# GpSimd's low part and division beside VectorE's block maxima, scales in one pass, column products in an earlier step

## The reference

```
Q = xn Wq^T + bq ; K = xn Wk^T + bk ; V = xn Wv^T + bv
Q, K divided by their norms over the 2048 tokens (per feature)
tailor = 1 / (256 + Q . (sum of K over features + 1e-6))
s = xn + gamma * tailor * (sum of V + Q (K^T V))          # linear attention
g = silu( ffn(xn) ),  ffn(x) = fp4_linear( silu(fp4_linear(x, w_gate)) * fp4_linear(x, w_up), w_down )
out = x + s * g
```

## Time and profile before

| | us |
|---|---|
| median of 3 runs | 691.5 |
| the three runs | 691.96, 686.57, 691.5 |
| the profiled execution | 686.41 |
| its span, first to last instruction | 684.5 |
| mean granted clock of PE | 0.984 |

### The profile page before, as it was taken

The page is one execution under the profiler, slowest core; times in us unless marked ns, Lnnn a source line. Parts: engine busy times, 40 slices in busy tenths (PEclk is TensorE's granted clock), DMA queues, the critical chain, the costliest instruction groups (busy, mean ns, idle before and its releaser), DMA issues.

```text
span 684.5 us, 14876 instructions
## 1 busy us (share of the span) xinstructions
PE 582.3 (85%) x4845; PEld 439.9 (64%) x4845; DVE 612.0 (89%) x1221; ACT 418.6 (61%) x1046; POOL 288.4 (42%) x224
## 2 busy tenths in 40 slices
PE   0247788999999699999999779999998889999767
PEld 0134566677768476777767656777776666777656
DVE  7987999999989999999989989999989998887634
ACT  3157887867667577766666567766667575553410
POOL 5424334443541335554752533554752443133315
PEclk9999999999999999999999999999999999999988
DMA  7001100000001001111101111111100110140123
GB/s 234 0 15 32 32 18 16 16 18 16 16 17 32 32 1 47 47 49 48 47 10 40 47 49 47 47 48 47 47 18 31 48 32 32 32 139 32 33 78 124
DMA packets 17758, 29.38 MB, mean 43 GB/s; under 512 B 2704, under 2 KB 5136, under 8 KB 17680
## 3 DMA queue, kind: packets, MB, share of 16 engines
q1 hardware_dynamic: 17680, 28.39, 12.5%
HBM read 19.99 MB, written 8.39 MB: 41 GB/s over the span
## 4 chain that ended last, share of the span: by engine, by line
DVE 48%; PE 25%; issue 18%; ACT 4%; POOL 2%; DMA 1%; DVEq 1%; SPq 0%; POOLq 0%; ACTq 0%
PE GU L1300 10%; DVE hg L863 5%; DVE h L823 5%; DVE hq L871 4%; DVE ham L830 4%; DVE hs L853 4%; PE G L1352 4%; DVE st L779 3%; PE DS L1311 3%; DVE xt L805 2%; DVE xq L814 2%; DVE y L882 2%; DVE ht L860 2%; DVE xg L808 2%; DVE xss L792 1%
## 5 line engine op out<-in xcount | busy, mean ns | idle before, releaser
L1300 PE MATMUL GU<-wgu,xqT 128*128 128x352 f16 x1536 | 256.5, 318 | 9.1 <-DVE h L823 4.6
L1300 PEld LDWEIGHTS GU<-wgu,xqT 128*128 128x128 f16 x1536 | 149.7, 100 | 85.5 <-ACT xnT L596 7.4
L520 POOL TENSOR_TENSOR ht<-h,hrr 128x1408 f32<-128x1408 f32 x32 | 82.9, 2590 | 238.7 <-DVE hrr L837 238.3
L580 ACT ACTIVATE sil<-GU,wkap 128x352 f32<-128x352 f32 x128 | 70.9, 555 | 105.0 <-PE GU L1300 103.2
L823 DVE SCALAR_TENSOR_TENSOR h<-GU,wkap,sil 128x352 f32<-128x352 f32 x128 | 72.0, 562 | 30.0 <-ACT sil L580 27.0
L1311 PE MATMUL DS<-wdT,hqT 128*128 128x256 f16 x704 | 88.2, 274 | 4.6 <-DVE y L882 3.3
L1311 PEld LDWEIGHTS DS<-wdT,hqT 128*128 128x128 f16 x704 | 66.7, 98 | 14.1 <-DVE y L882 3.3
L587 ACT COPY hqT<-TR 128x768 f16<-128x768 f16 x64 | 51.1, 798 | 32.6 <-PE TR L1258 32.0
L871 DVE TENSOR_TENSOR hq<-hg,hs 128x704 f16<-128x704 f16 x128 | 64.3, 544 | 1.0
L487 POOL TENSOR_TENSOR xt<-xs,xrr 128x512 f32<-128x512 f32 x32 | 43.5, 1360 | 42.2 <-DVE xrr L796 42.2
L1258 PE MATMUL TR<-id,hq 128*128 128x128 f16 x704 | 51.3, 220 | 7.9 <-ACT xnT L596 7.5
(11 more groups left out here) (181 smaller groups left out, 1095.8 us busy)
## 6 DMA issues: line engine op xcount, KB each, us to landing
xin<-in_L_attn_x SPq DMA_DIRECT2D x34, 256.0 KB, 2.7
xe<-in_L_attn_x SPq DMA_DIRECT2D x25, 256.0 KB, 2.9
out<-o SPq DMA_DIRECT2D x25, 256.0 KB, 2.1
h<-in_L_ffn_w_down SPq DMA_DIRECT2D x1, 704.0 KB, 6.5
gring<-in_L_ffn_w_gate SPq DMA_DIRECT2D x1, 640.0 KB, 4.5
gring<-in_L_ffn_w_up SPq DMA_DIRECT2D x1, 640.0 KB, 5.2
xs<-in_L_attn_x SPq DMA_DIRECT2D x2, 256.0 KB, 4.0
xt<-in_L_attn_x SPq DMA_DIRECT2D x2, 256.0 KB, 4.7
```

The lines of the kernel that those rows point to most:

```text
L520: g.tensor_tensor(paired(ht[:, 0:2 * I]), paired(h[:, q]), spread(hrr[:, q], 4 * CB), ALU.mult).then_inc(S["ht_d"], 1)
L580: a.activation(sil[:, c], GU[:, c, 0, 0:CH], ACT.Silu, scale=wkap[:, 0:1]).then_inc(S["sil_d"], 1)
L1300: last = t.matmul(GU[:, c, m, 0:CH], xqT[:, k, j, 2 * a_ + kc], wgu[:, b_, kc, 2 * m + c], start=(i == 0 and kc == 0), stop=(i == 2 and kc ...
```

## The change

Five edits:
- `h_high` (ScalarE) writes the scaled scales in f32 to a new tile `hsp` (still two operations of 44 columns), waits for them, and copies all 88 columns to `hs1`. VectorE's `h_parts(2)` is one operation hsp*1.0 - hs1 on 88 columns. Semaphore counts follow.
- POOL's `x_low` and `x_divide` go to the end of the iteration and wait for `hloq` = 2p, the last `hq` product of the iteration, behind which VectorE has the block maxima L830, then L834 and L837.
- POOL's `norm_products` run in step 3 (step 2 in the last batch), behind ht and ahead of o.
- `x_shift` is made by two ScalarE operations at the head of `x_norm`; VectorE's L792 moves behind the second `h` of the iteration, directly ahead of L796.
- "cols" is asked in (1, 0, 2) and answered in (1, 1, 0), in place of (3, 0, 0) and (3, 0, 1); turn moves to (1, 1, 1) and (1, 1, 2), t1q to (2, 0, 1), norms to (3, 1, 0). Waits of turn, cols and norms follow.

```diff
+        hsp = sb("hsp", [P, 2 * HB])
-        ASKS = {..., (1, 1, 0): "turn", (2, 0, 0): "t1q", (2, 1, 0): "t1k", (3, 0, 0): "cols", (3, 0, 2): "norms", ...
+        ASKS = {..., (1, 0, 2): "cols", (1, 1, 1): "turn", (2, 0, 1): "t1q", (2, 1, 0): "t1k", (3, 1, 0): "norms", ...
-        ANSWERS = {..., (1, 1, 1): "turn", (2, 0, 2): "t1q", (2, 1, 1): "t1k", (3, 0, 1): "cols", (3, 1, 1): "norms", ...
+        ANSWERS = {..., (1, 1, 0): "cols", (1, 1, 2): "turn", (2, 0, 2): "t1q", (2, 1, 1): "t1k", (3, 1, 1): "norms", ...
-        ASKS_END = {..., (1, 0, 1): "turn", ..., (2, 0, 2): "cols", ...
+        ASKS_END = {..., (1, 0, 1): "cols", (1, 1, 0): "turn", ...
-        ANSWERS_END = {..., (1, 1, 0): "turn", ..., (2, 1, 0): "cols", ...
+        ANSWERS_END = {..., (1, 0, 2): "cols", (1, 1, 1): "turn", ...
 # POOL, x_rstd
-                wait(pool, "rstd", u + 1)
-                wait(pool, "var_m", u + 1)
-                g.tensor_tensor(x_shift[:, :], nm[:, :], rs[:, :], ALU.mult).then_inc(S["nb_d"], 1)
 # POOL, iteration, behind ht
-                if on["xa"]:
-                    x_low(p, k)
-                    x_divide(p, k)
+                if i == (2 if last_batch else 3):
+                    norm_products(b)
                 if on["o"]:
...
                 if on["xf"]:
                     x_rstd(p + 1)
-                if i == 2:
-                    norm_products(b)
                 if i == (2 if last_batch else 3):
                     wait(pool, "nrm2", b + 1)
                     g.tensor_tensor(inv[:, :], nrm[:, :], half[:, :], ALU.pow).then_inc(S["inv_d"], 1)
+                if on["xa"]:
+                    if on["mb"]:
+                        wait(pool, "hloq", 2 * p)
+                    x_low(p, k)
+                    x_divide(p, k)
 # ScalarE, h_high
                 for j in range(2):
                     own = slice(j * HB, (j + 1) * HB)
-                    a.activation(hs1[:, q, own], hss[:, own], ACT.Copy, scale=hbq[:, j:j + 1]).then_inc(S["hs1_d"], 1)
+                    a.activation(hsp[:, own], hss[:, own], ACT.Copy, scale=hbq[:, j:j + 1]).then_inc(S["hsp_d"], 1)
+                wait(act, "hsp_d", 2 * u + 2)
+                wait(act, "hhiq", 2 * (u - 1))
+                a.copy(hs1[:, q], hsp[:, :]).then_inc(S["hs1_d"], 1)
 # ScalarE, x_norm
+                wait(act, "rstd", u + 1)
+                wait(act, "var_m", u + 1)
+                for j in range(2):
+                    last = a.activation(x_shift[:, j:j + 1], nm[:, j:j + 1], ACT.Copy, scale=rs[:, j:j + 1])
+                last.then_inc(S["nb_d"], 1)
                 wait(act, "nb_d", u + 1)
 # VectorE, h_parts(2)
-                    wait(dve, "hs1_d", 2 * u + 2)
-                    for j in range(2):
-                        own = slice(j * HB, (j + 1) * HB)
-                        v.scalar_tensor_tensor(hs2[:, q, own], hss[:, own], hbq[:, j:j + 1], hs1[:, q, own],
-                                               ALU.mult, ALU.subtract).then_inc(S["hs2_d"], 1)
+                    wait(dve, "hs1_d", u + 1)
+                    v.scalar_tensor_tensor(hs2[:, q], hsp[:, :], 1.0, hs1[:, q], ALU.mult, ALU.subtract).then_inc(S["hs2_d"], 1)
 # VectorE, iteration
-                if on["xa"]:
-                    x_scales(p, k, 1)
                 attention(0, 1)
                 if on["m"]:
                     h_mul(p, k, 0, 1)
                 if on["xa"]:
+                    x_scales(p, k, 1)
                     x_scales(p, k, 2)
 # PE: waits
 turn:   gram_e2 2b+2   ->  nrm1 b+1, row_ev b+1
 cols:   t1_ev 2b+2     ->  gram_e2 2b+2
 norms:  nrm1, row_ev   ->  t1_ev 2b+2     (prod_d 2b+2 stays)
```

More of the change, by code:

```diff
@@ L214, in build @@
             xlo xamax xss_d xrr_d xs1_d xs2_d xt_d xT_d xw_d xg_d xhiq xloq x_tr x_ev gu_d sil_d h_d ham_d
-            hss_d hrr_d hmx_d hbe_d hbq_d hs1_d hs2_d hun_d ht_d hT_d hw_d hg_d hhiq hloq hA_tr hB_tr hA_ev
+            hss_d hrr_d hmx_d hbe_d hbq_d hsp_d hs1_d hs2_d hun_d ht_d hT_d hw_d hg_d hhiq hloq hA_tr hB_tr hA_ev
             hB_ev down_d g_d s_d y_d o_d xe_in0 xe_in1 xend_in out_d0 out_d1 wamax wmaxd wmax_tr wtopd walld wbet wkapd wssd wrrd
@@ L262, in spread_in_order @@
             return ap.rearrange("p (n e o) -> p n e o", o=1, e=2).broadcast_to([P, blks // 2, 2, BLK])
-        ASKS = {(-1, 1, 2): "gram0_first", (0, 0, 1): "gram0_last", (0, 1, 2): "gram1", (1, 1, 0): "turn",
-                (2, 0, 0): "t1q", (2, 1, 0): "t1k", (3, 0, 0): "cols", (3, 0, 2): "norms", (3, 1, 2): "raw",
+        ASKS = {(-1, 1, 2): "gram0_first", (0, 0, 1): "gram0_last", (0, 1, 2): "gram1", (1, 0, 2): "cols",
+                (1, 1, 1): "turn", (2, 0, 1): "t1q", (2, 1, 0): "t1k", (3, 1, 0): "norms", (3, 1, 2): "raw",
                 (4, 0, 2): "tailor", (4, 1, 2): "product", (5, 1, 0): "top", (5, 1, 2): "high_low", (6, 0, 1): "row"}
-        ANSWERS = {(0, 1, 0): "gram0", (1, 0, 0): "sums", (1, 0, 1): "gram1", (1, 1, 1): "turn", (2, 0, 2): "t1q",
-                   (2, 1, 1): "t1k", (3, 0, 1): "cols", (3, 1, 1): "norms", (4, 0, 1): "raw", (4, 1, 0): "tailor",
+        ANSWERS = {(0, 1, 0): "gram0", (1, 0, 0): "sums", (1, 0, 1): "gram1", (1, 1, 0): "cols", (1, 1, 2): "turn",
+                   (2, 0, 2): "t1q", (2, 1, 1): "t1k", (3, 1, 1): "norms", (4, 0, 1): "raw", (4, 1, 0): "tailor",
                    (5, 0, 1): "product", (5, 1, 1): "top", (6, 0, 0): "high_low", (6, 0, 1): "row"}
-        ASKS_END = {(-1, 1, 2): "gram0_first", (0, 0, 0): "gram0_last", (0, 1, 0): "gram1", (1, 0, 1): "turn",
-                    (1, 1, 1): "t1q", (2, 0, 0): "t1k", (2, 0, 2): "cols", (2, 1, 1): "norms", (3, 0, 0): "raw",
+        ASKS_END = {(-1, 1, 2): "gram0_first", (0, 0, 0): "gram0_last", (0, 1, 0): "gram1", (1, 0, 1): "cols",
+                    (1, 1, 0): "turn", (1, 1, 1): "t1q", (2, 0, 0): "t1k", (2, 1, 1): "norms", (3, 0, 0): "raw",
                     (3, 0, 2): "tailor", (3, 1, 1): "product", (4, 0, 0): "top", (5, 1, 2): "high_low_row"}
-        ANSWERS_END = {(0, 0, 2): "gram0", (0, 1, 2): "gram1", (1, 0, 0): "sums", (1, 1, 0): "turn", (1, 1, 2): "t1q",
-                       (2, 0, 1): "t1k", (2, 1, 0): "cols", (2, 1, 2): "norms", (3, 0, 1): "raw", (3, 1, 0): "tailor",
+        ANSWERS_END = {(0, 0, 2): "gram0", (0, 1, 2): "gram1", (1, 0, 0): "sums", (1, 0, 2): "cols", (1, 1, 1): "turn",
+                       (1, 1, 2): "t1q", (2, 0, 1): "t1k", (2, 1, 2): "norms", (3, 0, 1): "raw", (3, 1, 0): "tailor",
                        (3, 1, 2): "product", (4, 0, 1): "top", (5, 1, 2): "high_low_row"}
@@ L656, in h_high @@
                 wait(act, "hbe_d", u + 1)
-                wait(act, "hs2_d", 2 * u)
+                wait(act, "hs2_d", u)
                 a.activation(hbq[:, :], hbe[:, :], ACT.Copy, scale=HTOP).then_inc(S["hbq_d"], 1)
@@ L662, in h_high @@
                 wait(act, "hbq_d", u + 1)
-                wait(act, "hhiq", 2 * (u - 1))
                 for j in range(2):
                     own = slice(j * HB, (j + 1) * HB)
-                    a.activation(hs1[:, q, own], hss[:, own], ACT.Copy, scale=hbq[:, j:j + 1]).then_inc(S["hs1_d"], 1)
+                    a.activation(hsp[:, own], hss[:, own], ACT.Copy, scale=hbq[:, j:j + 1]).then_inc(S["hsp_d"], 1)
+                wait(act, "hsp_d", 2 * u + 2)
+                wait(act, "hhiq", 2 * (u - 1))
+                a.copy(hs1[:, q], hsp[:, :]).then_inc(S["hs1_d"], 1)
             def x_norm(p, k):
                 u, q = p + LEADA, (k + LEADA) % 2
+                wait(act, "rstd", u + 1)
[3 more added lines that the diff above has]
+                last.then_inc(S["nb_d"], 1)
                 wait(act, "nb_d", u + 1)
@@ L867, in h_round @@
                     wait(dve, "hg_d", u + 1)
-                    wait(dve, "hs2_d", 2 * u + 2)
+                    wait(dve, "hs2_d", u + 1)
                     wait(dve, "hB_tr", 2 * (u - 1))
@@ L1356, in ask @@
                 if step == "turn":
-                    wait(pe, "gram_e2", 2 * b + 2)
+                    wait(pe, "nrm1", b + 1)
+                    wait(pe, "row_ev", b + 1)
                     for k in range(KD):
@@ L1373, in ask @@
                 if step == "cols":
-                    wait(pe, "t1_ev", 2 * b + 2)
+                    wait(pe, "gram_e2", 2 * b + 2)
                     wait(pe, "sum_ev", b + 1)
@@ L1384, in ask @@
                 if step == "norms":
-                    wait(pe, "nrm1", b + 1)
-                    wait(pe, "row_ev", b + 1)
+                    wait(pe, "t1_ev", 2 * b + 2)
                     wait(pe, "prod_d", 2 * b + 2)
```

## The result

The changed kernel took 706.1 us (median of 4 runs, 700.21 to 714.43) against 689.9 us for the kernel before (also 4 runs). The longest of its runs, 714.43 us, counts as a slow one and is left out of the ratio, which is 1.021 with a 95% interval of 1.011 to 1.031; the other three have a median of 703.2 us. That is slower by about 2%, and by both medians outside the predicted range of 674 to 700 us.

What follows compares the result with a forecast made beforehand. VectorE was taken to bound steps 3, 5, 6 and the early iterations, PE mostly the rest. Terms -4.8, -3.4, -4.0, -0.5, +4.9 and +3.6 came to -4.2 us, giving 687.3 us, range 674 to 700.

Steps and rivals of the forecast that it cites:

- Part 2: x_low and x_divide behind the last hq: hss loses 0.55 us; L792 behind the second h waits 0.9 us in step -1.
- Part 5: Shift and copy on ScalarE: 0.35 us ahead of the gate; steps -1 and 0 both taken as 0.
- the terms -4.8 and -3.4: Step 5 shorter by 1.8 us twice and 1.2 once; step 6 by 1.5 us twice and 0.4 once.
- The early term, -4.0: Early iterations without attention work: three shorter by 1.2 us each, the fourth by 0.4 us.
- the ten terms that held it: Gains in steps 5, 6 and early iterations, each less 0.55 us for hss waiting until x_divide ends.
- Part 1: L853 as one operation without a column operand takes 0.25 us, gaining 2.0 or 1.0 us per iteration.
- Part 4: Column products from step 3 to step 1: +1.75 us in two middle batches, +1.4 in the first, +4.9 in all.
- Part 3: norm_products from step 2 to step 3: 4.7 us lost, 3.5 saved there, net +1.2 us three times, +3.6.
- B: Rival, chance 0.20: PE and ScalarE's gate close the loop in every iteration; +8.3 us, 699.8 us.
- A: Rival, chance 0.28: the short VectorE operations hardly wait for POOL; 674 us.
- C: Rival, chance 0.08: new waits of equal length replace the old in each iteration; 691.5 us, no change.

Runs made afterwards that it cites:

- e5: Changed kernel with L792 (the x scales) back ahead of the answers and the second h: 691.7 us, 1.005.
- e7: Changed kernel with L792 back, tables and norm_products as before, x_divide waiting for hss, step 2's x_low and x_divide behind ht: 679.6 us, 0.985.
- e8: Kernel before with only POOL's x_low and x_divide moved behind the last hq, x_divide waiting for hss, step 2 unmoved: 668.5 us, 0.971.
- e11: e8 without x_divide's wait for hss: 675.2 us, 0.982.
- e2: Changed kernel with x_divide made to wait for hss of the same iteration: 696.2 us, 1.010.
- e3: Changed kernel with both ScalarE edits undone, so no copy, two low-scale operations on VectorE, x_shift on POOL: 704.7 us, 1.022.
- e10: e8 plus hsp and its copy on ScalarE and one low-scale operation on VectorE: 679.1 us, 0.987.
- e1: Kernel before with only the attention tables and PE's waits of the changed kernel: 697.7 us, 1.011.
- e12: e8 plus the changed kernel's tables and place of norm_products, with x_low and x_divide late in step 2 too: 679.5 us, 0.987.
- e9: e8 plus x_shift made by two ScalarE operations: 671.3 us, 0.976.
- e4: Changed kernel with x_low and x_divide back directly behind ht, ahead of norm_products: 712.2 us, 1.033.

## Why the prediction was wrong

In medians the way from the changed kernel to the fastest is: L792 back, -14.4 us (e5; -11.5 from the 703.2 us); tables, norm_products and the wait for hss, -12.1 (e7); ScalarE's edits out, -11.0 (e8). The remaining edit, POOL's move, is then worth 668.5 - 689.7 = -21 us with the wait for hss, and 675.2 - 690.0 = -15 us without it (e11). The prediction had the edit that gains, and priced the ones that lose mainly by what they do on VectorE.

**Part 2, moved L792: the failed step.** It was priced as VectorE's wait of 0.9 us for POOL in step -1, and at nothing "where an answer or an idle stands ahead (1, 4, 5, 6)". On VectorE that is right: L801 takes 0.17 us in step 5. But the answers and `h` ahead of it are a delay of its result, and ScalarE's x_high stands ahead of h_abs and the gate on its queue. Part 5 saw that L792 can delay the gate, but took for it only the 0.9 us wait for POOL, in step -1, and counted 0. In step 5 x_high starts 9.14 - 5.77 = 3.4 us later (table). Price: 11 to 14 us in the changed kernel, 6.4 alone. With it the terms -4.8 and -3.4 (steps 5 and 6) fall: their pieces grew by 2.2 and 0.7 us in the last full batch.

The early term, -4.0, fell for another reason. The four early pieces, 61.2 us together before, are 60.5 in the changed kernel. With L792 back they are no shorter (61.6, e5); with x_divide behind hss they are 59.4 (e2), and with ScalarE's edits out 58.1 (e3). In e8, POOL's move alone, they are 57.4, and steps 5 and 6 are 17.64 and 17.09 in place of 19.15 and 18.86: there the predicted gains of both terms stand, without the merge.

**Part 2, hss.** The mechanism was right. L843 takes 0.76 us in the early iterations and 0.99 later, in place of 0.21; the 0.55 us fits the early ones only. In the steady ones x_low starts 0.40 us into the maxima (500.61 against 500.21) and not 0.17 us, and x_divide ends later by as much. The rule that spoke against the edit (the Trainium skill, "SBUF — State Buffer", "Who interferes with whom": a `tensor_scalar` in a two-port mode is blocked for the whole of a GpSimd operation, a `tensor_reduce` never) agrees with the trace: the maxima keep 1.61 us beside POOL's operations, and L843 ends as x_divide does (502.85 and 502.78). What failed is "Where VectorE sits idle after L837 (steps 1, 4) it costs nothing": hss feeds hmx, hbe, h_high and so the gate. e2 gives 7 to 10 us for it, e11 6.7 us, where the ten terms that held it came to 10 x 0.55 = 5.5 us.

**Part 1.** L860 takes 0.24 us in the median, as predicted (0.25). The saving was put down to the merge, though; e8 has it without (0.30 us mean, two operations, 52.6 to 16.6 us together). It belongs to POOL's move.

**Part 5, the copy: taken as 0, bounds 0 and 0.35 us plus L792's delay.** It was not hidden: the gate comes 0.32 us later. In the changed kernel it cost nothing that e3 could show, as the wait for L801 is longer. Without that wait it costs 10.6 us (e10), and not evenly: of the 10.5 us that e10 is longer from its first to its last maxima, 4.5 stand in three pieces, and in each of these PE's clock fell behind the wait for the gate (2.05, 2.31 and 2.05 us), where e8 waited 1.69, 1.51 and 1.69 us at full clock. The 39% idle of ScalarE was no evidence: most of it lies ahead of `sil` and `hqT` (65.2 and 23.1 us of the 370 us read), and 13.2 us ahead of the gate.

**Part 4, columns.** Middle batches: +1.6 in e1 against +1.75 foreseen for steps 1 and 2, and +0.5 on e8 (e12). In the changed kernel steps 0 to 2 went from 17.44 + 19.51 + 18.78 = 55.73 to 57.54 us, +1.81, but 1.3 of it is step 0, which e8 also has at 18.72 us without the tables. That 1.81 is so near to 1.75 is chance, and step 0, taken as 0, was wrong. First batch +3.4 (e1) against +1.4. Last batch: foreseen -0.5, measured +2.3 in e1 and +6.4 in the changed kernel, of which 2.3 is again step 0 (e10 has it too). The prediction walked the tables of the middle batches and not the `_END` ones, where turn, t1q and the columns stand closer together. Whole part: about +8 us (e1), and +10.9 with part 3 (e12).

**Part 3, norm_products.** Step 3 grew by 0.55 us (predicted 1.2) in the batch where nothing else disturbs it, and by 1.8 and 2.7 in the other two. The alternation was as foreseen. VectorE beside POOL in step 3 of the changed kernel:

```profile
506.44 1.13 DVE L801 TENSOR_SCALAR xss<-xam 128x32 f32<-128x32 f32 x1
...
507.88 1.01 DVE L814 SCALAR_TENSOR_TENSOR xt<-xT,xt 128x512 f32<-128x512 f32 x1
508.81 1.31 DVE L860 SCALAR_TENSOR_TENSOR hs<-hsp,hs 128x88 f16<-128x88 f32 x1
```
```profile
506.27 1.27 POOL L504 TENSOR_TENSOR wqkv<-HLs,wqT 128x512 f32<-128x512 f32 x1
507.62 0.73 POOL L506 TENSOR_TENSOR wqkv<-wqkv 128x256 f32<-128x256 f32 x1
508.31 1.71 POOL L504 TENSOR_TENSOR wqkv<-As,wkT 128x512 f32<-128x512 f32 x1
510.10 1.21 POOL L506 TENSOR_TENSOR wqkv<-wqkv 128x256 f32<-128x256 f32 x1
511.27 2.76 POOL L533 TENSOR_TENSOR o<-y,xe 128x512 f32<-128x512 f32 x1
```
L801 ends at 507.57 as the first product does (507.54), L860 at 510.12 after the second (510.02).

**The rivals.** B named the right loop (PE and ScalarE's gate) and came nearest, 699.8 against 706.1, with the wrong thing in it: 0.35 us of copy an iteration, where the moved x scales and hss hold the gate back. Its deciding point came true: PE's idle in steps 5 and 6 shrank from 5.3 and 3.8 to 4.55 and 3.05 us, and nearly all of it is now the wait for the gate (4.55 and 2.60 us, before 1.95 and 1.70):

```profile
573.52 0.87 PE L1339 MATMUL DS<-Mx,xnT 128*128 128x256 f16 x6 [2.60 <-ACT gring L625]
```
But B left these pieces as long as they were, and they grew. A and C fall: hss does wait, and the time changed.

## What to carry to other kernels

When an operation moves later, price its result and not only the operation: find the engine that reads it, and walk that engine's in-order queue to the first wait that ends last. Here one line on VectorE held back all that stood behind its reader on ScalarE, and then PE: 11 to 14 us. And before an operation that is slow beside another engine is rewritten, move the other engine: the slow pair was 3 times faster with no edit of its own, and the rewrite's one small copy lay on the way to the gate.

## What the runs showed of the hardware

PE's granted clock often falls after it has waited, and this multiplies small delays. In step 5 of the changed kernel it is 0.50 for the 4.6 us behind a wait of 4.55 us. In step 6 of e10 it fell behind a wait of 2.05 us (0.62 over the next 4.5 us) and in e8 it did not behind 1.69; in the kernel before a wait of 1.95 us left the next products at full speed. The length of one wait does not decide it: at one and the same place (the wait for `kap` near 230 us) e9 waited 2.48 us and had 0.60 over the next 4 us, while e8 waited 2.49 us and kept 1.00. The changed kernel kept 1.00 even behind a wait of 3.53 us (at 238.37). Behind waits at the lower level 12 gate and up products take 2.97 to 3.68 us in place of 1.95 (3.68 in e4 above). The changed kernel's profiled execution spent 65 us at half clock and the kernel before 24. If PE bounded all of these 41 us more, at 1 - 1.95/3.68 = 0.47 lost of each, that would be 19 us (an estimate, and an upper one) of the 28 between these two executions. How much is this and how much the waits themselves was not separated.

POOL's operations grow beside VectorE's as VectorE's do beside POOL's: the output sum o takes 2.76 us in step 3 above where it took 1.27, and L504 1.71 in place of 1.28, while VectorE's two-input operations run.
